# Projections: half of the values' product in front of the queries' product, and VectorE's low part of the queries in front of the moments

## What is computed

```python
t = to_tokens(x)                                  # 16 x 1024 x 128
z = (t - mean(t)) / sqrt(var(t) + 1e-5)           # _ln_t, over the channels
x = (z - mu) / sqrt(var + LN_EPS) * ln_gamma + ln_beta
q = x @ Wq + bq                                   # and + u_bias
k = x @ Wk + bk
v = x @ Wv + bv
```

## Time and profile before

| | us |
|---|---|
| median of 3 runs (3747.4 to 3750.81) | 3750.76 |
| profiled execution | 3750.45 |
| its span | 3748.6 |
| TensorE busy in the span | 3103.8 |
| VectorE busy | 2722.6 |
| ScalarE busy | 2198.8 |
| GpSimd busy | 704.1 |

### The profile page before, as it was taken

The page is one execution under the profiler, slowest core; times in us unless marked ns, Lnnn a source line. Parts: engine busy times, 40 slices in busy tenths (PEclk is TensorE's granted clock), DMA queues, the critical chain, the costliest instruction groups (busy, mean ns, idle before and its releaser), DMA issues. The chain is left out here.

```text
span 3748.6 us, 76712 instructions
## 1 busy us (share of the span) xinstructions
PE 3103.8 (83%) x29428; PEld 2368.4 (63%) x29428; DVE 2722.6 (73%) x5210; ACT 2198.8 (59%) x3568; POOL 704.1 (19%) x760
## 2 busy tenths in 40 slices
PE   3798888889757588888888888889888883999994
PEld 2565665656446367677677667677676772777773
DVE  4778787787544367887888888888888883776674
ACT  2455555555444367666667766667666661777670
POOL 1000000000011100212112212112212203566661
PEclk8999999999877789999999999999999996999995
DMA  2355463544458799999999999999999993777776
GB/s 59 111 176 146 145 190 111 184 131 154 155 208 316 235 354 368 363 372 370 360 373 368 380 369 366 363 370 377 369 373 378 366 339 118 245 252 256 251 228 270
DMA packets 290943, 1023.22 MB, mean 273 GB/s; under 512 B 51620, under 2 KB 57520, under 8 KB 281574
## 3 DMA queue, kind: packets, MB, share of 16 engines
q1 hardware_dynamic: 273382, 985.62, 74.7%
q0 software_dynamic: 17280, 33.87, 2.4%
HBM read 486.25 MB, written 489.85 MB: 260 GB/s over the span
## 5 line engine op out<-in xcount | busy, mean ns | idle before, releaser
L954 ACT ACTIVATE att_skewed<-att_skewed,att_neg_max 128x1024 f32<-128x1024 f32 x512 | 589.0, 1150 | 422.7 <-DVE att_neg_max L1095 422.4
L1095 DVE CUSTOM_DVE_ANT_0 att_skewed<-att_score_ps,att_skewed 128x1024 f32<-128x1024 f32 x512 | 625.5, 1222 | 124.5 <-issue 107.3
L1211 PE MATMUL att_turn_ps<-att_ident,att_skewed 128*128 128x128 f32 x4096 | 577.8, 286 | 142.2 <-ACT att_skewed L954 140.8
L1211 PEld LDWEIGHTS att_turn_ps<-att_ident,att_skewed 128*128 128x128 f32 x4096 | 471.4, 145 | 324.1 <-ACT att_skewed L954 302.9
L945 ACT ACTIVATE att_rows<-att_wide_ps 128x1152 f32<-128x1152 f32 x512 | 573.3, 1120 | 128.2 <-PE att_wide_ps L1175 127.8
L1103 DVE COPY att_turned<-att_turn_ps 128x1024 f32<-128x1024 f32 x512 | 624.7, 1220 | 10.5 <-PE att_turn_ps L1211 9.8
L1175 PE MATMUL att_wide_ps<-att_ps,att_qs 98*128 98x128 f32 (+3 forms) x1920 | 435.3, 348 | 23.6 <-DVE att_token L987 17.1
L909 POOL DMA_INDIRECT expert_rows<-att_expert_rows,att_place x256 | 247.9, 968 | 814.2 <-DVE att_place L1053 727.3
L1203 PE MATMUL att_score_ps<-att_ks,att_qs 96*128 96x512 f32 x1024 | 368.9, 442 | 35.9 <-DVE att_neg_max L1095 33.2
L1175 PEld LDWEIGHTS att_wide_ps<-att_ps,att_qs 98*128 98x128 f32 x1920 | 311.0, 201 | 77.3 <-issue 33.2
L155 POOL DMA_INDIRECT expert_parts<-exp_parts,exp_rows x284 | 299.1, 1053 | 206.9 <-ACT exp_parts L186 140.9
(11 more groups left out here) (263 smaller groups left out, 5193.8 us busy)
## 6 DMA issues: line engine op xcount, KB each, us to landing
skewed_rows<-att_rows SPq DMA_DIRECT2D x512, 576.0 KB, 7.1
att_skewed<-skewed_rows SPq DMA_DIRECT2D x512, 512.0 KB, 7.4
expert_rows<-conv_pad SPq DMA_DIRECT2D x144, 520.0 KB, 11.1
exp_weights<-split_weights SPq DMA_DIRECT2D x71, 1028.0 KB, 6.9
att_qs<-queries SPq DMA_DIRECT2D x192, 128.0 KB
att_ks<-keys SPq DMA_DIRECT2D x192, 128.0 KB
exp_rows<-expert_rows SPq DMA_DIRECT2D x71, 260.0 KB, 3.0
sum_part<-expert_parts SPq DMA_DIRECT2D x32, 512.0 KB, 7.5
```

Of the source, the lines that this page charges most:

```text
L954: act.activation(skewed[r % RING][:], skewed[r % RING][:], ACT.Exp, bias=neg_max[:, k:k + 1], scale=-1.0, accum_out=sums[:, k:k + 1]).then ...
L1095: dve.tensor_tensor_reduce(skewed[r % RING][:], score_ps[:], skewed[r % RING][:], -SCALE, 3.0e38, ALU.add, ALU.min, neg_max[:, k:k + 1]).t ...
L1211: last = pe.transpose(turn_ps[:, t * P:(t + 1) * P], skewed[r % RING][:, t * P:(t + 1) * P], ident[:])
```

## The change

TensorE's half of it: `values` takes a range of tiles. The first four of eight tiles are now computed at the start of a turn, in front of the queries' product, and the other four where all eight were, in front of the keys' product. The wait for `v_read` goes with the first tile, the signal `v_filled` with the last. VectorE's half: `low(n-1, 0)`, which makes `ql`, is now in front of `moments(n+1)`. ScalarE's, GpSimd's and SyncE's queues are as they were.

```diff
@@ -572,10 +572,10 @@
             moments(0)
             offsets(0)
             for n in range(NB + 1):
+                if n:
+                    low(n - 1, 0)
                 if n + 1 < NB:
                     moments(n + 1)
-                if n:
-                    low(n - 1, 0)
                 if n < NB:
                     dve.wait_ge(z_high, n + 1)
                     dve.tensor_tensor(zl[n % 2][:], z_ps[:], raw(zh[n % 2][:]), ALU.subtract).then_inc(z_low, 1)
@@ -623,26 +623,28 @@
-            def values(n):
-                if n:
+            def values(n, tiles):
+                if n and tiles[0] == 0:
                     pe.wait_ge(v_read, n)
-                for t in range(TT):
+                for t in tiles:
                     cut = slice(t * P, (t + 1) * P)
                     for k, (a, z) in enumerate(terms(n)):
                         last = pe.matmul(v_ps[:, cut], z[:, cut], a[:, 2, :], start=(k == 0), stop=(k == 2))
-                last.then_inc(v_filled, 1)
+                if tiles[-1] == TT - 1:
+                    last.then_inc(v_filled, 1)
 
             tokens(0)
             for n in range(NB + 1):
                 if n:
                     pe.wait_ge(z_low, n)
+                    values(n - 1, range(TT // 2))
                     project(n - 1, 0)
                 if n + 1 < NB:
                     tokens(n + 1)
                 if n < NB:
                     channels(n)
                 if n:
-                    values(n - 1)
+                    values(n - 1, range(TT // 2, TT))
                     project(n - 1, 1)
```

## The result

The changed kernel takes 3738.52 us, median of 20 runs, beside 3752.52 for the kernel before over as many. The ratio is 0.9957, with a 95% interval of 0.9944 to 0.997: 0.43% faster, 11 to 21 us. The profiled execution has a span of 3736.0 us for 3748.6, 12.6 less. That 3738.52 lies so near the forecast of 3738 is partly luck: the kernel before came out at 3752.52 here and not at the 3750.76 that the forecast started from, so the gain is some 14 to 16 us and not 12.6.

A forecast was written before the change was run, and what follows sets the result against it. It took in-order VectorE, standing twice on the projections' path, and in the middle SyncE's queue, to bound the phase. Terms of -2.0, -3.4, -1.3, -5.9 and nothing sum to -12.6 us: 3738 us from 3750.76, range 3731 to 3747.

The forecast's parts named there:

- The path through VectorE: Projections: the path runs queries, tokens, moments, `ql`, keys, `kh`, `kl`, standing on in-order VectorE twice; reordered, 9.93 us for 10.76.
- the sum: An undisturbed turn added up from one `kl`: `ql` 4.24, moments 5.43, `offsets` 9.84, next `kl` 9.93 us.
- The wait for `rstd`: In front of `offsets` on VectorE: GpSimd's `rstd`, covered then by `zl` alone, leaves some 0.4 us idle in most turns.
- Turn 1: Early projections: the moved half of the values' product has no cover, costing 0 to 2.6 us; +0.5 taken.
- Turns 2 and 3: Early projections: 23.1 us becomes 10.7 + 9.9; together with turn 1's +0.5, -2.0.
- Late turns: Five late projection turns: 58.4 us becomes 11.1 + 3 x 10.7 + 9.3, a gain of 5.9.
- The middle: Seven turns held by SyncE's queue: -3.4 us from its waits for computation, and -1.3 in the last of them.
- rival (a): Transfers hold the middle: stores crowd, the 3.4 us vanish, late turns stay at 11.2; -7.7, 3743 us; chance 0.19.
- The last turn: End of the projections: `ql` takes the values' place, 8.43 us for 8.4, so nothing gained.
- (c): TensorE stays at 1.2 GHz through whole turns, 14.3 us each in early and late turns; 3764 us; chance 0.07.
- rival (b): TensorE's waits simply go, 1.8 us a turn, VectorE's chain being looser; turns of 9.0, -17, 3734 us; chance 0.08.

The follow-up runs named there:

- experiment 5: Changed kernel plus 12 overwritten matmuls a turn, filling TensorE's idle time in front of the wait for `zl`: ratio 0.9946 to the kernel before.
- experiment 1: Changed kernel with only TensorE's half (half of the values' product in front), VectorE's order as before: ratio 0.9977 to the kernel before.
- experiment 2: Changed kernel with only VectorE's half (`ql` in front of the moments), the whole values' product where it was: ratio 0.9974 to the kernel before.
- experiment 7: GpSimd's power made twice: added to the changed kernel, ratio 1.0018; added to the kernel before, ratio 0.9989, both to the kernel before.
- experiment 9: SyncE's staging of the next weights one iteration later: in the changed kernel 3708.41 us, ratio 0.9872; in the kernel before, ratio 0.9932.
- experiment 6: Kernel before plus 24 overwritten matmuls a turn in front of the queries' product, filling idle time: 3738.18 us, ratio 0.995.
- experiment 3: Changed kernel again without any edit, timed and profiled a second time: ratio 0.9958 to the kernel before.
- before_stage_late: Kernel before with SyncE's staging of the next weights one iteration later, compute order unchanged: ratio 0.9932 to the kernel before.

## Why the prediction came true

**The path through VectorE: right.** Turn by turn the sum holds within 0.05 us (experiment 5), and both halves alone behave as the sum has them (10.8 and 10.1 us, experiments 1 and 2). The wait for `rstd` is what closes the cycle: doubled, it lengthens the changed kernel's turns and not those before (experiment 7). It is 0.62 us and not 0.43, because in the earlier trace rows `zl` itself started 0.20 later for want of `zh`, and so stood in the wait; from the moments to `offsets` it is 4.41 there and 4.40 here.

**Turn 1: right.** +0.5 was said, 0.3 came in both profiles against the first profile of the kernel before, whose second had 18.5 (0.7 less). **Turns 2 and 3: right between two profiles.** -2.5 was said; -1.9 and -3.4 came, with granted clocks of 0.84 and 1.00.

**Late turns: right, with the clock as assumed.** -5.9 was said; -6.2 and -5.0 came. The three without weights took 10.4 to 11.0 in the first profile and 10.8 to 11.5 in the second, for the 10.7 said. The first, with its weights, took 10.55 both times for 11.1.

**The middle: wrong by most of its 3.4 + 1.3.** -2.8 came in the first profile, +1.4 in the second, against the first of the kernel before. The step that failed is "I take 3.4, since the nearest rows show SyncE free and waiting". SyncE's waits for `weights_l` at L457 did go from the middle (none is left between 1088 and 1203, for 3.4 us in the first profile of the kernel before and only 1.0 in its second), but the waits for its own stores grew. They were

```profile
SPq L446 <- DMA split_weights<-proj_staged: 37.9, 6, 8.6
```

in the kernel before, 38.6 in its second profile, and in the changed kernel

```profile
SPq L446 <- DMA split_weights<-proj_staged: 40.2, 6, 8.6
```

and 42.9 in its second: 2.3 and 4.3 us more, about what the other wait gave up in the first profile. Stagings came every 16.5 us on average (five intervals, 1101.20 to 1183.94) for 16.9 (1102.15 to 1186.62), 2 us in all. That is the first half of rival (a): the weight stores took longer, a median of 8.3 us from issue to landing in both profiles of the changed kernel (`weights_l`, 1088 to 1203) for 6.7 and 7.4 in the kernel before. But the transfers as such don't hold the middle, as (a) has it: experiment 9 moved the wait out of the way and the middle fell by 25 us. The other half of (a), late turns without weights at 11.2, came in the second profile (11.5, 10.8, 11.1, with clocks of 0.72 to 0.85) and not in the first (10.4, 10.6, 11.0). The DMA that ends the wait isn't one that no engine's order shortens, as the prediction says, since the order in SyncE's own queue did.

**The last turn: a term of nothing that was +1.1** in the first profile (queries at 1.2 GHz, and the keys' product waited 0.84 for `ql`) and 0 in the second. I had put both orders at 2.4 GHz.

**A count that was off.** In (c) the prediction puts TensorE's work at 7.3 us a turn; by the earlier trace rows it is 7.7 (10.76 less 2.61 and 0.43), so the idle time should fall to 2.2, not to 2.6. No term of the sum rests on it.

**The total.** The sum of 12.6 us equals the difference of the two first spans by chance: that pair has 9.5 of it in the phase and 3.1 in phases that the change doesn't touch. The better figure for the phase is the 11.4 of two profiles each. In it the middle gives 1.2 for the 4.7 said, and the last turn 1.5 for nothing said, the latter only because the kernel before spent 12.6 us on it, at 1.2 GHz, in one of its two profiles.

**The rivals.** The kernel's time alone, 11 to 21 us faster, doesn't part the forecast from rival (b) with its 17; the turns do. (b) is out: no turn with tokens came near 9.0 in any kernel, and even with the clock at 1.00 they are 9.86. (c) is out: the late mean clock was 0.87 for 0.86, and in the second profile one turn of five was under 0.75. Yet its mechanism was the right one to fear. How much the clock matters here, experiment 6 shows: filling the idle time of the old order gave as much as the new order did. What separates the two is that the new order doesn't use the filler and ends at 9.9 instead of 10.8 once the clock is up (experiments 3, 5 and 9). What decides whether it is up stays open: the last turns of the changed kernel's two profiles have the same idle time of 1.24 us in front of the queries' product, and a pair of it took 1.14 us in one and 0.73 in the other.

## What to carry to other kernels

Where an in-order engine stands on the path twice in a turn, write the cycle out from one of its instructions to the same one of the next turn; moving matmuls into a gap left the undisturbed turn at 10.8 us until the engine that ends the gap was moved too. Ask of each step that moves what it used to cover: here a small power on GpSimd came onto the path. And before counting gains in a stretch whose loads hang on one DMA queue, move the queue's blocking wait behind its other work: this gave 30 us where the compute order had given 14 to 16.

## What the runs showed of the hardware beyond what I expected

Redundant matmuls can pay for themselves: with 24 a turn in the old order, overwritten at once, the mean granted clock of the late turns was 0.97 for 0.86, and the kernel 13 to 24 us faster (experiment 6). With 12 in the new order it was 1.00 for 0.87, but there the time gained isn't clear of noise (experiment 5). Idle time of 1.6 to 2.15 us in front of each queries' product went with 1.2 GHz at its start in all undisturbed turns (experiment 7), and yet 2.61 us went with 2.4 GHz in turn 3 of the kernel before: the length of the gap alone doesn't tell the clock behind it. The kernel before with the later staging was at 0.83 to 0.86 in all 15 turns (experiment 9, before_stage_late), while other profiles of the same order have turns at 1.00. The phase of the kernel before differed by 6.4 us between two profiles of the same program, 4.1 of it in the last turn, where values and keys ran at 1.2 GHz in one of them.
